# Quantised self-attention: row maxima turned and split group by group, first exponentials behind group 0 alone, the last group's maximum scores taken head by head between steps, one value bank in PSUM, the rounding of v on GpSimd

## The chip, the cores and the metric

The kernel is one program for one of the eight cores of a Trainium2 chip. The metric is the device time of one execution in microseconds. A core has TensorE (PE in the rows; its weight loads are PEld), VectorE (DVE), ScalarE (ACT), GpSimd (POOL) and SyncE (SP), each with its own queue of instructions, run in order. They meet on semaphores: an instruction adds to one with `then_inc`, another engine stands still at `wait_ge` until the count is there.

## What is computed

The block is cross-attention, then quantised self-attention, then a mixture of experts, on x of 8 x 128 tokens by 512. Only the middle part matters here:

```python
def _L0_attn_ref(query, key, value, in_w, in_b, out_w, out_b):   # query = layernorm(x), key and value unused
    X = fake_quant(einsum('lbe,fe->lbf', query, fake_quant(in_w)) + in_b)
    Q, K, V = split(X, 3, axis=-1)          # 16 heads of 32; L = 8, B = 128
    ...
    q = fake_quant(q / sqrt(HD))
    attn = softmax(einsum('bqd,bkd->bqk', q, k))
    heads = fake_quant(einsum('bqk,bkd->bqd', attn, v))
    y = heads_r @ Wo.T + out_b
    return fake_quant(y)
```

`fake_quant` divides by the largest absolute value of the whole tensor over 127, rounds, and multiplies back. Attention runs over L = 8 positions, for each of 128 batch rows and 16 heads apart.

## The kernel before

`quantised_self_attention` holds the stage. The 16 heads are in G = 4 groups f of GH = 4 heads j; one group fills the 128 partitions, 32 to a head. q and k lie transposed in `qk` (8 chunks of 128 x 1024: q of group f in chunk f, k in chunk 4 + f), v in `v_val` (8 tiles of 128 x 512, all groups side by side). PSUM, TensorE's output memory, is used as `pa` and `pb`, four banks of 128 x 512 each; `pt[0]` and `pt[1]` are banks 2 and 3 of `pb`.

The work between the scale of X (`x_scaled`) and the largest head value goes in two phases.

- **Maxima.** A group is quantised: k by two DVE instructions (`quantise_k`), q of groups 0 to 2 by four ACT instructions each, q of group 3 by four DVE instructions (`quantise_q`). `scores_for_max(f)` writes the mask (`half_l` by `half_r`) and 64 small matmuls into four banks (`pa` for even f, `pb` for odd), and DVE takes the largest score of each row, 128 x 2048 elements, into `mx`. After all four groups PE turns `mx` over (`m_turned`), and DVE splits it into `m_hi` and `m_lo`, two fp16 parts (`m_split`).
- **Steps.** s goes from 0 to 7; step s treats group s // 2, half s % 2 of its tokens. `scores_transposed(s)` writes mask, scores and minus the maximum into all of `pa`; ACT takes the exponential (2048 columns, `probs[s % 2]`); `times_v(s)` multiplies by v into bank s % 2 of `pb`, and ACT copies it to `heads` (`copy_heads`); `denominators(s)` sums the probabilities into `pt[0]`; DVE inverts (`invert`); `widen(s)` spreads the inverse over `pt[1]`; DVE multiplies and takes the largest (`normalise`).

The order of the work is written out by hand. PE runs `scores_transposed(s + 1)`, `times_v(s)`, `denominators(s)`, `widen(s - 1)` in each step. GpSimd rounds v of tiles 4 to 7 once three k groups are there (`v_late`), ACT those of tiles 0 to 3 after its q groups (`v_ready`).

Of the kernel before, what the change touches and what calls it, by code (L numbers as in the profile page):

```python
# [6 lines left out]
f16 = mybir.dt.float16  # L7
# [7 lines left out]
P = 128  # L15
# [3 lines left out]
EC = D // P  # L19
# [1157 lines left out]
def quantised_self_attention(nc, weights_q, wscale, in_b, out_b, w1, w2, stage, stage_in, shared, x1, x1_stats, ident, ident16):  # L1177
# [7 lines left out]
    with ExitStack() as c:  # L1185
# [26 lines left out]
        m_hi = sb("m_hi", [P, P], f16)  # L1212
        m_lo = sb("m_lo", [P, P], f16)
# [32 lines left out]
        v_ready, v_late = sem("v_ready2"), sem("v_late2")  # L1246
# [23 lines left out]
        with nc.Block() as block:  # L1270
# [11 lines left out]
            def _(gp):  # L1282
# [35 lines left out]
                gp.wait_ge(k_ready, G - 1)  # L1318
                for n, g in enumerate(range(4, B)):
                    gp.tensor_scalar(v_val[:, g, :], v_val[:, g, :], inv["x"][:, :], ROUND, ALU.mult, ALU.add).then_inc(v_late, 1)  # L1320
                    gp.wait_ge(v_late, 2 * n + 1)
                    gp.tensor_scalar(v_val[:, g, :], v_val[:, g, :], -ROUND, 1.0, ALU.add, ALU.mult).then_inc(v_late, 1)
# [8 lines left out]
            def _(act):  # L1331
# [19 lines left out]
                for f in range(G - 1):  # L1351
                    q_f = qk[:, f, :]
                    act.activation(q_f, q_f, ACT.Identity, bias=up, scale=inv["x"][:, :]).then_inc(q_step, 1)
                    act.wait_ge(q_step, 3 * f + 1)
                    act.activation(q_f, q_f, ACT.Identity, bias=down).then_inc(q_step, 1)
                    act.wait_ge(q_step, 3 * f + 2)
                    act.activation(q_f, q_f, ACT.Identity, bias=up, scale=scale["xq"][:, :]).then_inc(q_step, 1)
                    act.wait_ge(q_step, 3 * f + 3)
                    act.activation(q_int[:, f, :], q_f, ACT.Identity, bias=down).then_inc(q_ready, 1)

                for n in range(2):
                    v_n = v_val[:, 2 * n:2 * n + 2, :]
                    act.activation(v_n, v_n, ACT.Identity, bias=up, scale=inv["x"][:, :]).then_inc(v_ready, 1)
                    act.wait_ge(v_ready, 2 * n + 1)
                    act.activation(v_n, v_n, ACT.Identity, bias=down).then_inc(v_ready, 1)

                def copy_heads(s):
                    act.wait_ge(pv_done, s + 1)
                    act.activation(heads[:, s // 2, tokens(s)], pb[:, s % 2, :], ACT.Copy, scale=scale["x"][:, :]).then_inc(head_copied, 1)
# [24 lines left out]
            def _(dve):  # L1394
# [29 lines left out]

                split_xt(2)
# [42 lines left out]
                def quantise_k(f):  # L1468
                    k_f = qk[:, EC + f, :]
                    dve.tensor_scalar(k_f, k_f, inv["x"][:, :], ROUND, ALU.mult, ALU.add).then_inc(k_step, 1)  # L1470
                    dve.wait_ge(k_step, f + 1)
# [8 lines left out]

                quantise_k(0)
                quantise_k(1)
                quantise_k(2)
                for f in range(G):
                    if f == 1:
                        quantise_q(G - 1)
                    if f == 2:
                        quantise_k(G - 1)
                    dve.wait_ge(m_ready, f + 1)
                    dve.tensor_reduce(mx[:, :, 8 * f:8 * f + 8], (pa, pb)[f % 2][:, :, :].rearrange("p j (i n) -> p j i n", n=B * HT),  # L1490
                                      AX.X, ALU.max).then_inc(m_read, 1)

                dve.wait_ge(m_turned, 1)
                do(dve.tensor_scalar(m_round[:, :], pt[0][:, 0:P], 1.0 / 512.0, ROUND, ALU.mult, ALU.add))
                do(dve.tensor_scalar(m_hi[:, :], m_round[:, :], -ROUND, 1.0, ALU.add, ALU.mult))
                dve.scalar_tensor_tensor(m_lo[:, :], m_hi[:, :], -512.0, pt[0][:, 0:P], ALU.mult, ALU.add).then_inc(m_split, 1)
# [61 lines left out]
            def _(pe):  # L1558
# [48 lines left out]

                def scores_for_max(f):
                    out = (pa, pb)[f % 2]
                    pe.wait_ge(mask_ready, 1)  # L1610
                    if f >= 2:
                        pe.wait_ge(m_read, f - 1)
                    for j in range(GH):
                        rows = slice(HD * j, HD * j + HT + 1)
                        pe.matmul(out[:, j, :], half_l[rows, :], half_r[rows, :].unsqueeze(1).to_broadcast([HT + 1, 8, B * HT]),
# [805 lines left out]
```

## Time and profile before

| what | us |
|---|---|
| median of 3 runs | 1738.03 |
| the three runs | 1733.03, 1738.48, 1738.03 |
| the profiled execution | 1731.91 |
| its span (first to last instruction) | 1730.2 |
| from the scale of X (1166.05) to the largest head value (1228.19) | 62.1 |
| of that, before the first exponential (1189.81) | 23.8 |

The profiled execution is one run, 1.7 us longer than the span that the trace covers. A time such as 1189.81 is counted from the span's start. A row's idle time is that of the engine just before the instruction; it costs something only where the engine is the one for which all others wait.

### The profile page before, as it was taken

What the parts mean: (1) busy time and instruction counts of PE and PEld (TensorE: products, weight loads), DVE (VectorE), ACT (ScalarE), POOL (GpSimd) and SP (SyncE); (2) the same over time, 40 slices, a digit from 0 to 9 for tenths busy, and PEclk for the clock granted to TensorE, in tenths of its full rate; (3) what the DMA queues carried; (4) which work ended last, traced back from release to release, by engine and by line L of the source; (5) the groups of instructions that cost most, each with busy time, mean ns of one, the idle gap of its engine ahead of it and who ended that gap; (6) DMA issues with size and microseconds to landing.
All of it is one profiled execution on the core that took longest, in us unless ns stands there. A gap on an engine that the chain in (4) does not pass through costs nothing. (4 is left out here: it accounts for less than half of the span.)

```text
span 1730.2 us, 39796 instructions
## 1 busy us (share of the span) xinstructions
PE 1621.8 (94%) x17262; PEld 1109.3 (64%) x17262; DVE 1166.7 (67%) x1388; ACT 774.5 (45%) x979; POOL 466.9 (27%) x404
## 2 busy tenths in 40 slices
PE   6999999999999999999999999886569999999996
PEld 4666666666666666666766666664347777777774
DVE  5678568568567657657656766566787667666766
ACT  5355336335344444445435435447535344444441
POOL 2323312232232123123212247531024411101133
PEclk9999999999999999999999999996879999999998
DMA  6534343243234234233232235450048655645534
GB/s 245 126 108 111 68 108 86 62 123 86 47 98 111 47 87 114 56 87 92 59 105 74 57 87 141 104 209 3 2 140 279 203 180 182 201 171 181 192 127 110
DMA packets 102151, 202.04 MB, mean 117 GB/s; under 512 B 25739, under 2 KB 25739, under 8 KB 101850
## 3 DMA queue, kind: packets, MB, share of 16 engines
q1 hardware_dynamic: 91258, 169.49, 33.5%
q0 software_dynamic: 10720, 30.02, 6.1%
q8 instruction: 137, 2.24, 0.5%
q14 instruction: 36, 0.29, 0.0%
HBM read 127.36 MB, written 18.90 MB: 85 GB/s over the span
## 5 line engine op out<-in xcount | busy, mean ns | idle before, releaser
L656 DVE TENSOR_REDUCE mx<-sc 128x4 f32<-128x2048 f32 x128 | 293.1, 2290 | 65.4 <-PE sc L900 64.8
L861 PE MATMUL proj<-w_hi,ctx 128*128 128x256 f16 x2048 | 273.5, 278 | 12.6 <-ACT ctx L441 12.5
L489 ACT ACTIVATE stage_w<-sc 128x1024 f32<-128x1024 f32 x256 | 248.2, 1025 | 69.2 <-PE sc L935 68.5
L875 PE MATMUL proj<-ctx,w_hi 128*128 128x512 f16 x1024 | 253.6, 380 | 0.0
L861 PEld LDWEIGHTS proj<-w_hi,ctx 128*128 128x128 f16 x2048 | 193.2, 99 | 64.5 <-issue 40.1
L452 ACT ACTIVATE stage_w<-proj 128x512 f32<-128x512 f32 x128 | 76.4, 597 | 339.3 <-PE proj L861 339.3
L383 POOL TENSOR_TENSOR acc_g<-stage_w 128x1024 f32<-128x1024 f32 x31 | 74.0, 2389 | 472.2 <-ACT stage_w L489 472.1
L678 DVE TENSOR_TENSOR acc_v<-acc_v,stage_w 128x1024 f32<-128x1024 f32 x93 | 129.6, 1394 | 87.2 <-ACT stage_w L489 84.4
L1166 DVE SCALAR_TENSOR_TENSOR w_lo<-stage_w,w_hi 128x2048 f16<-128x2048 f32 x64 | 144.8, 2293 | 35.2 <-ACT w_hi L1160 35.1
L616 DVE SCALAR_TENSOR_TENSOR k_lo<-proj,k_hi 128x512 f16<-128x512 f32 x128 | 87.9, 687 | 117.9 <-ACT k_hi L461 117.0
L875 PEld LDWEIGHTS proj<-ctx,w_hi 128*128 128x128 f16 x1024 | 90.0, 98 | 116.5 <-issue 25.1
L861 PE MATMUL proj<-w_lo,ctx 128*128 128x256 f16 x1024 | 157.1, 277 | 1.2 <-DVE w_lo L604 1.2
L1947 ACT ACTIVATE hf<-ph 128x321 f32<-128x321 f32 x128 | 56.3, 440 | 208.1 <-PE ph L2220 190.5
L2236 PE MATMUL po<-h_lo,w_hi 128*128 128x321 f16 x496 | 149.3, 301 | 0.0
L2236 PE MATMUL po<-h_hi,w_hi 128*128 128x321 f16 x496 | 149.2, 301 | 0.0
L2236 PE MATMUL po<-h_hi,w_lo 128*128 128x321 f16 x496 | 149.2, 301 | 0.0
L935 PEld LDWEIGHTS sc<-qs,stage_w 97*128 97x128 f16 x2048 | 125.2, 98 | 31.2 <-ACT stage_w L489 2.5
L935 PE MATMUL sc<-qs,stage_w 97*128 97x128 f16 x2048 | 136.7, 220 | 3.8 <-DMA stage_w<-k_hi 1.6
L952 PE MATMUL po<-stage_w 128*32 128x128 f32 x4096 | 139.2, 277 | 0.0
L875 PE MATMUL proj<-ctx,w_lo 128*128 128x512 f16 x512 | 131.8, 380 | 0.0
L461 ACT ACTIVATE k_hi<-proj 128x512 f16<-128x512 f32 x128 | 76.5, 597 | 105.0 <-PE proj L875 101.8
L388 POOL TENSOR_TENSOR acc_g<-acc_g,stage_w 128x1024 f32<-128x1024 f32 x31 | 81.8, 2640 | 151.9 <-ACT stage_w L489 151.9
(344 smaller groups left out, 2492.5 us busy)
## 6 DMA issues: line engine op xcount, KB each, us to landing
stage_w<-in_w SPq DMA_DIRECT2D x64, 1024.0 KB, 5.6
ctx_stage<-in_ctxT SPq DMA_DIRECT2D x64, 512.0 KB, 4.4
stage_w<-k_hi SPq DMA_DIRECT2D x256, 128.0 KB, 2.4
stage_w<-k_lo SPq DMA_DIRECT2D x128, 128.0 KB, 2.4
wq_f<-in_wiT POOLq DMA_DIRECT2D x24, 256.0 KB, 4.2
xg<-xbuf POOLq DMA_DIRECT2D x28, 176.0 KB, 4.3
obuf<-o_sb POOLq DMA_DIRECT2D x28, 176.0 KB, 3.5
xbuf<-final SPq DMA_DIRECT2D x17, 256.0 KB
```

The source lines that it names most:

```text
L388: gp.tensor_tensor(acc_g[:, :], acc_g[:, :], probs[:, 3, :], ALU.add).then_inc(sum_g, 1)
L461: act.activation(k_hi[:, 512 * kb:512 * kb + 512], proj[where % 2][:, :], ACT.Copy, scale=1.0 / WSCALE).then_inc(proj_act, 1)
L489: act.activation(probs[:, u % 4, :], unit_scores(u), ACT.Exp, scale=1.0 / sqrt(HD)).then_inc(e_ready, 1)
L616: dve.scalar_tensor_tensor(k_lo[part], proj[where % 2][:, :], 1.0 / WSCALE, k_hi[part], ALU.mult, ALU.subtract).then_inc(k_low, 1)
L656: dve.tensor_reduce(mx[:, :, kb], sc[:, :, :], AX.X, ALU.max).then_inc(m_read, 1)
L678: dve.tensor_tensor(acc_v[:, :], acc_v[:, :], probs[:, (0, 0, 1, 2)[part], :], ALU.add).then_inc(sum_v, 1)
L861: last = pe.matmul(out, x_part[:, kb, e, col:col + P], w_part[:, 2, e, wv], start=term == 0 and e == 0, stop=term == 2 and e == EC - 1)
L875: last = pe.matmul(proj[at % 2][:, :], w_part[:, 1, e, P * (g % G):P * (g % G) + P], x_part[:, kb, e, :], start=term == 0 and e == 0, stop ...
L935: last = pe.matmul(sc[:, 2 * (u % 2) + i, P * j:P * j + P], ks[0:QKM, j, P * ck:P * ck + P], qs[0:QKM, 4 * g + j, :], start=True, stop=True)
L952: last = pe.matmul(po[HD * j:HD * j + HD, 0:T], v_sb[:, g // 2, ck, at:at + HD], probs[:, u % 4, 512 * i + P * j:512 * i + P * j + P], sta ...
L1166: dve.scalar_tensor_tensor(w_lo[:, s % NSPLIT], stage[:, s], WSCALE, w_hi[:, s % NSPLIT], ALU.mult, ALU.subtract).then_inc(stage_lo, 1)
L2236: last = pe.matmul(po[i][:, 0:CAP], w_part[:, s % NSPLIT, f, P * i:P * i + P], h_part[:, at, :], start=q == 0 and f == 0 and n == 0, stop= ...
```

## The change

The same values are computed, in another order and partly on other engines.

- DVE quantises q of group 0, then k of group 1; ACT quantises k of group 0, then q of groups 1 and 2. q and k of group 3 follow on DVE after the maxima of group 2.
- `mx` is set to zero at the start of the stage, and is turned and split three times (`turn_largest`, `split_largest`): after group 0, after group 2, after group 3. The parts go to two slots in the free region `xt2`.
- `scores_transposed(0)` and with it the first exponential wait for the first split alone. The maximum scores of groups 1 and 2 use `pb` (no longer two sets of banks in turn).
- The maximum scores of group 3 are made for one head at a time in one bank, `pb[:, 1]`, by 1 + 16 matmuls (`last_scores_for_max`), in the steps s = 1, 2, 3 and 4; DVE reads each by a 128 x 512 maximum (`largest_of_last`).
- `times_v` uses bank 0 of `pb` in every step, so it waits until the heads of the step before are copied.
- GpSimd rounds all eight tiles of v, as soon as q of group 0 is quantised; ACT none.

```diff
@@ GpSimd
-                gp.wait_ge(k_ready, G - 1)
-                for n, g in enumerate(range(4, B)):
+                gp.wait_ge(k_ready, 1)
+                for g in range(B):
...
@@ ScalarE
-                for f in range(G - 1):
+                k_0 = qk[:, EC, :]
+                act.activation(k_0, k_0, ACT.Identity, bias=up, scale=inv["x"][:, :]).then_inc(q_step, 1)
+                act.wait_ge(q_step, 1)
+                act.activation(k_int[:, 0, :], k_0, ACT.Identity, bias=down).then_inc(q_ready, 1)
+                for n, f in enumerate((1, 2)):
...
-                for n in range(2):
-                    v_n = v_val[:, 2 * n:2 * n + 2, :]
-                    act.activation(v_n, v_n, ACT.Identity, bias=up, scale=inv["x"][:, :]).then_inc(v_ready, 1)
-                    act.wait_ge(v_ready, 2 * n + 1)
-                    act.activation(v_n, v_n, ACT.Identity, bias=down).then_inc(v_ready, 1)
@@ VectorE
+                def largest_scores(f):
+                    dve.wait_ge(m_ready, f + 1)
+                    dve.tensor_reduce(mx[:, :, 8 * f:8 * f + 8], (pa, pb)[f > 0][:, :, :].rearrange("p j (i n) -> p j i n", n=B * HT),
+                                      AX.X, ALU.max).then_inc(m_read, 1)
+
+                def largest_of_last(j):
+                    dve.wait_ge(m_ready, G + j)
+                    dve.tensor_reduce(mx[:, j, 8 * G - 8:8 * G], pb[:, 1, :].rearrange("p (i n) -> p i n", n=B * HT),
+                                      AX.X, ALU.max).then_inc(m_read, 1)
+
+                def split_largest(n):
+                    turned = (pa[:, 0, 0:P], pb[:, 1, 0:P])[n > 0]
+                    dve.wait_ge(m_turned, n + 1)
+                    do(dve.tensor_scalar(m_round[:, :], turned, 1.0 / 512.0, ROUND, ALU.mult, ALU.add))
+                    do(dve.tensor_scalar(m_hi[:, n % 2, :], m_round[:, :], -ROUND, 1.0, ALU.add, ALU.mult))
+                    dve.scalar_tensor_tensor(m_lo[:, n % 2, :], m_hi[:, n % 2, :], -512.0, turned, ALU.mult, ALU.add).then_inc(m_split, 1)
...
+                quantise_q(0)
                 quantise_k(1)
+                largest_scores(0)
+                split_largest(0)
+                largest_scores(1)
                 quantise_k(2)
...
+                largest_scores(2)
+                quantise_k(G - 1)
+                split_largest(1)
+                quantise_q(G - 1)
...
                 for s in range(NS):
+                    if s == 4:
+                        largest_of_last(3)
                     invert(s)
+                    if 1 <= s < 4:
+                        largest_of_last(s - 1)
+                    if s == 4:
+                        split_largest(2)
                     if s:
                         normalise(s - 1)
@@ TensorE
+                def own_positions(out, j):
+                    rows = slice(HD * j, HD * j + HT + 1)
+                    pe.matmul(out, half_l[rows, :], half_r[rows, :].unsqueeze(1).to_broadcast([HT + 1, 8, B * HT]),
+                              start=True, stop=False, tile_position=(HD * j, 0))
+
+                def half_scores(out, f, i, h, j):
+                    at = slice(P * i + 64 * h, P * i + 64 * h + 64)
+                    rows = slice(HD * j, HD * j + HD)
+                    return pe.matmul(out[64 * h:64 * h + 64, 64 * i:64 * i + 64], q_int[rows, f, at],
+                                     k_int[rows, f, at], start=False, stop=i == 7, tile_position=(HD * j, 64 * h))
...
+                def last_scores_for_max(j):
+                    pe.wait_ge(m_read, 3 + j)
+                    if j == 0:
+                        pe.wait_ge(m_split, 2)
+                        pe.wait_ge(k_ready, G + 1)
+                    own_positions(pb[:, 1, :], j)
+                    for i in range(8):
+                        for h in range(2):
+                            last = half_scores(pb[:, 1, :], G - 1, i, h, j)
+                    last.then_inc(m_ready, 1)
+
+                def turn_largest(out, known):
+                    pe.wait_ge(m_read, known)
+                    pe.transpose(out, mx[:, :, :].rearrange("p j i -> p (j i)"), ident[:, :]).then_inc(m_turned, 1)
...
                     pe.wait_ge(e_ready, s + 1)
                     if s == 0:
-                        pe.wait_ge(v_ready, 4)
-                    if s == 1:
-                        pe.wait_ge(v_late, 8)
-                    if s >= 2:
-                        pe.wait_ge(head_copied, s - 1)
+                        pe.wait_ge(m_read, 3)
+                    else:
+                        pe.wait_ge(head_copied, s)
+                    if s < 2:
+                        pe.wait_ge(v_ready, B * (s + 1))
...
+                scores_for_max(0)
+                turn_largest(pa[:, 0, 0:P], 1)
+                scores_for_max(1)
                 scores_transposed(0)
+                scores_for_max(2)
                 for s in range(NS):
                     if s + 1 < NS:
                         scores_transposed(s + 1)
+                    if s == 0:
+                        turn_largest(pb[:, 1, 0:P], 3)
+                    if s == 4:
+                        last_scores_for_max(3)
                     times_v(s)
                     denominators(s)
+                    if 1 <= s < 4:
+                        last_scores_for_max(s - 1)
+                    if s == 4:
+                        turn_largest(pb[:, 1, 0:P], G + 3)
                     if s:
                         widen(s - 1)
```

On PE, from the maxima to the first step, the rows stood so before (`half_r,half_l` is the mask of `scores_for_max`, `k_int,wo_sb` its 64 matmuls, since q's integers lie in `wo_sb`; `ident,mx` is the turn; `mask_r,mask_l` opens `scores_transposed(0)`):

```order
L1615 MATMUL pa<-half_r,half_l 128x512 x4
L1625 MATMUL pa<-k_int,wo_sb 64x64 x64
L1615 MATMUL pb<-half_r,half_l 128x512 x4
L1625 MATMUL pb<-k_int,wo_sb 64x64 x64
L1615 MATMUL pa<-half_r,half_l 128x512 x4
L1625 MATMUL pa<-k_int,wo_sb 64x64 x64
L1615 MATMUL pb<-half_r,half_l 128x512 x4
L1625 MATMUL pb<-k_int,wo_sb 64x64 x64
L1692 MATMUL pb<-ident,mx 128x128
L1605 MATMUL pa<-mask_r,mask_l 128x512 x4
```

On PE at the same place they stand so in the changed kernel:

```order
L1626 MATMUL pa<-half_r,half_l 128x512 x4
L1632 MATMUL pa<-k_int,wo_sb 64x64 x64
L1663 MATMUL pa<-ident,mx 128x128
L1626 MATMUL pb<-half_r,half_l 128x512 x4
L1632 MATMUL pb<-k_int,wo_sb 64x64 x64
L1621 MATMUL pa<-mask_r,mask_l 128x512 x4
```

The turn and the first step have moved ahead of groups 2 and 3; after the step's matmuls come mask and 64 matmuls of group 2, and nothing of group 3.

On DVE, from the first k to the split of the maxima, these rows stood before (`ctx` is `qk`; L1470 and L1472 quantise k, L1476 to L1479 q of group 3, L1490 is the maximum of a group, L1494 to L1496 the split):

```order
L1470 TENSOR_SCALAR ctx<-ctx,inv_x 128x1024
L1472 TENSOR_SCALAR k_int<-ctx 128x1024 [waits k_step]
L1490 TENSOR_REDUCE mx<-pa 128x4x8 [waits m_ready2]
L1476 TENSOR_SCALAR ctx<-ctx,inv_x 128x1024
L1477 TENSOR_SCALAR ctx<-ctx,scale_xq 128x1024 [waits v_step2]
L1478 TENSOR_SCALAR ctx<-ctx 128x1024 [waits v_step2]
L1479 TENSOR_SCALAR wo_sb<-ctx 128x1024 [waits v_step2]
L1490 TENSOR_REDUCE mx<-pb 128x4x8 [waits m_ready2]
L1470 TENSOR_SCALAR ctx<-ctx,inv_x 128x1024
L1472 TENSOR_SCALAR k_int<-ctx 128x1024 [waits k_step]
L1490 TENSOR_REDUCE mx<-pa 128x4x8 [waits m_ready2]
```

In the changed kernel DVE's rows at that place are these (L1475 to L1478 quantise q of group 0, L1469 and L1471 k of group 1, L1482 is a group's maximum, L1493 to L1495 the split):

```order
L1475 TENSOR_SCALAR ctx<-ctx,inv_x 128x1024
L1476 TENSOR_SCALAR ctx<-ctx,scale_xq 128x1024 [waits v_step2]
L1477 TENSOR_SCALAR ctx<-ctx 128x1024 [waits v_step2]
L1478 TENSOR_SCALAR wo_sb<-ctx 128x1024 [waits v_step2]
L1469 TENSOR_SCALAR ctx<-ctx,inv_x 128x1024
L1471 TENSOR_SCALAR k_int<-ctx 128x1024 [waits k_step]
L1482 TENSOR_REDUCE mx<-pa 128x4x8 [waits m_ready2]
L1493 TENSOR_SCALAR xn<-pa 128x128 [waits m_turned]
L1494 TENSOR_SCALAR ctx_stage<-xn 128x128 [waits v_step2]
L1495 SCALAR_TENSOR_TENSOR ctx_stage<-ctx_stage,pa 128x128 [waits v_step2]
L1482 TENSOR_REDUCE mx<-pb 128x4x8 [waits m_ready2]
```

A group's q has moved ahead of everything, and a split stands between the first and the second maximum. Behind these rows DVE still has k of group 2, the maximum of group 2, k of group 3, the second split and q of group 3, and then the first `invert`.

In a step (here s = 1) PE has two rows more than before, those of `last_scores_for_max(0)` between the denominators (`probs,every`) and `widen` (`ot,ident`):

```order
L1701 MATMUL pb<-probs,v_val 32x128 x16
L1712 MATMUL pb<-probs,every 32x128 x16
L1626 MATMUL pb<-half_r,half_l 128x512
L1632 MATMUL pb<-k_int,wo_sb 64x64 x16
L1724 MATMUL pb<-ot,ident 32x128 x16
L1621 MATMUL pa<-mask_r,mask_l 128x512 x4
```

The mask is one matmul here and the scores sixteen, all with the rows of one head.

## Rows read from the trace of the kernel before

**Rows 1.** The page, parts 1 and 2: share of the span; 40 slices in tenths.

```profile
PE 1621.8 (94%) x17262; PEld 1109.3 (64%) x17262; DVE 1166.7 (67%) x1388; ACT 774.5 (45%) x979; POOL 466.9 (27%) x404
PEclk9999999999999999999999999996879999999998
```

**Rows 2.** Windows: stretch, length, busy us (instructions) by engine, PEclk, DMA share, GB/s.

```profile
1166.00:1188.00 22.00, 6.07 (x277) 3.51 (x281) 20.01 (x24) 19.96 (x17) 6.23 (x8) 0.50 0.01 1
1188.00:1198.00 10.00, 7.92 (x196) 6.05 (x192) 0.63 (x1) 4.54 (x3) 0.00 (x0) 0.51 0.01 2
1198.00:1228.00 30.00, 27.61 (x1004) 22.79 (x992) 17.89 (x24) 15.96 (x13) 0.00 (x0) 1.00 0.02 5
```

**Rows 3.** Timeline of the maxima: start, length, engine, line, what; idle before it, and releaser.

```profile
1166.05 1.24 ACT L1353 ACTIVATE ctx<-ctx,rounds_up,inv_x 128x1024 f32<-128x1024 f32 x1 [18.39 <-DVE scale_qx L1459]
1166.83 0.75 DVE L1470 TENSOR_SCALAR ctx<-ctx,inv_x 128x1024 f32<-128x1024 f32 x1
...
1171.07 0.79 PE L1625 MATMUL pa<-k_int,wo_sb 32*64 32x64 f16 x64 [3.68 <-ACT wo_sb L1359]
...
1171.80 0.61 PE L1615 MATMUL pb<-half_r,half_l 9*128 9x512 bf16 x4
1171.90 2.29 DVE L1490 TENSOR_REDUCE mx<-pa 128x32 f32<-128x2048 f32 x1 [0.81 <-PE pa L1625]
...
1180.37 1.23 ACT L1363 ACTIVATE v_val<-v_val,rounds_up,inv_x 128x1024 f32<-128x1024 f32 x1
...
1184.08 2.28 DVE L1490 TENSOR_REDUCE mx<-pb 128x32 f32<-128x2048 f32 x1
1185.10 1.28 ACT L1375 ACT_TABLE_LOAD   x1
...
1186.42 0.47 PE L1692 MATMUL pb<-ident,mx 128*128 128x128 f32 x1 [3.60 <-DVE mx L1490]
...
1187.86 0.61 PE L1605 MATMUL pa<-mask_r,mask_l 17*128 17x512 bf16 x4 [0.97 <-DVE m_lo L1496]
```

**Rows 4.** Groups by line and shape, 1166 to 1188: count, busy us, mean ns.

```profile
L1320 POOL TENSOR_SCALAR v_val<-v_val,inv_x 128x512 f32<-128x512 f32 x4 | 3.2, 803 | 21.3 <-DVE k_int L1472 21.3
L1322 POOL TENSOR_SCALAR v_val<-v_val 128x512 f32<-128x512 f32 x4 | 3.1, 774 | 0.3
L1470 DVE TENSOR_SCALAR ctx<-ctx,inv_x 128x1024 f32<-128x1024 f32 x4 | 3.0, 746 | 0.0
L1472 DVE TENSOR_SCALAR k_int<-ctx 128x1024 f16<-128x1024 f32 x4 | 2.8, 694 | 0.1
...
L1476 DVE TENSOR_SCALAR ctx<-ctx,inv_x 128x1024 f32<-128x1024 f32 x1 | 1.1, 1142 | 0.0
L1478 DVE TENSOR_SCALAR ctx<-ctx 128x1024 f32<-128x1024 f32 x1 | 1.1, 1066 | 0.0
```

**Rows 5.** Timeline of the first two steps.

```profile
1189.81 1.97 ACT L1375 ACTIVATE probs<-pa,scale_qx 128x2048 f32<-128x2048 f32 x1 [3.42 <-PE pa L1645]
1191.83 0.61 PE L1605 MATMUL pa<-mask_r,mask_l 17*128 17x512 bf16 x4 [2.08 <-ACT probs L1375]
...
1193.65 1.94 PE L1661 MATMUL pb<-probs,v_val 128*32 128x128 f32 x32
...
1197.23 0.61 PE L1605 MATMUL pa<-mask_r,mask_l 17*128 17x512 bf16 x4
...
1198.45 1.08 PE L1661 MATMUL pb<-probs,v_val 128*32 128x128 f32 x32
...
1199.35 1.06 PE L1672 MATMUL pb<-probs,every 128*32 128x128 f32 x32
```

**Rows 6.** Timeline, a later step, and the last row of the steps.

```profile
1204.33 0.68 ACT L1369 ACTIVATE ctx<-pb,scale_x 128x512 f32<-128x512 f32 x1
...
1206.23 1.08 PE L1661 MATMUL pb<-probs,v_val 128*32 128x128 f32 x32
...
1227.47 0.69 DVE L1414 TENSOR_REDUCE tile_max<-ctx 128x1 f32<-128x512 f32 x1
```

More of the change, by code:

```diff
@@ L1423, in largest_qk @@
                     absmax(tile_max[:, j // 2, 2 * c + j % 2:2 * c + j % 2 + 1], of_pairs(qk[:, 2 * j:2 * j + 2, :], c), AX.XY)
+                steps.did(dve.memset(mx[:, :, :], 0.0))
                 split_xt(2)
@@ L1608, in scores_for_max @@
                 def scores_for_max(f):
-                    out = (pa, pb)[f % 2]
+                    out = (pa, pb)[f > 0]
                     pe.wait_ge(mask_ready, 1)
-                    if f >= 2:
-                        pe.wait_ge(m_read, f - 1)
+                    if f == 2:
+                        pe.wait_ge(m_read, 2)
                     for j in range(GH):
-                        rows = slice(HD * j, HD * j + HT + 1)
-                        pe.matmul(out[:, j, :], half_l[rows, :], half_r[rows, :].unsqueeze(1).to_broadcast([HT + 1, 8, B * HT]),
-                                  start=True, stop=False, tile_position=(HD * j, 0))
@@ L1617, in scores_for_max @@
-                    pe.wait_ge(k_ready, f + 1 if f < G - 1 else G + 1)
-                    if f < G - 1:
-                        pe.wait_ge(q_ready, f + 1)
+                        own_positions(out[:, j, :], j)
+                    pe.wait_ge(k_ready, f + 1)
+                    pe.wait_ge(q_ready, f + 1)
                     for i in range(8):
                         for h in range(2):
-                            at = slice(P * i + 64 * h, P * i + 64 * h + 64)
                             for j in range(GH):
-                                rows = slice(HD * j, HD * j + HD)
-                                last = pe.matmul(out[64 * h:64 * h + 64, j, 64 * i:64 * i + 64], q_int[rows, f, at],
-                                                 k_int[rows, f, at], start=False, stop=i == 7, tile_position=(HD * j, 64 * h))
+                                last = half_scores(out[:, j, :], f, i, h, j)
@@ L1646, in scores_transposed @@
                                                  pick[rows, n, HD * j + at:HD * j + at + 1].to_broadcast([HD, P]),
-                                                 m_part[rows, :], start=False, stop=i == 3 and n == 1, tile_position=(HD * j, 0))
+                                                 m_part[rows, (0, 1, 1, 0)[s // 2], :], start=False, stop=i == 3 and n == 1, tile_position=(HD * j, 0))
                     last.then_inc(s_ready, 1)
@@ L1660, in times_v @@
                             at = P * (s // 2) + HD * j
-                            last = pe.matmul(pb[HD * j:HD * j + HD, s % 2, P * i:P * i + P],
+                            last = pe.matmul(pb[HD * j:HD * j + HD, 0, P * i:P * i + P],
                                              v_val[:, 4 * (s % 2) + i, at:at + HD],
```

43 lines of the change are left out of this document (15 added, 28 removed).

## The prediction

> **What bounds the kernel now.** I read the page first. TensorE is busy for 94% of the span, and its clock stands at the full level of 2.4 GHz except around slice 28 [rows 1]. A stretch in which PE is not the limit is there, and it is the one changed. The windows put numbers on it: from 1166 to 1188 PE works 6.1 of 22 us at half clock (0.50, which is 1.2 GHz), while VectorE has 20.0 and ScalarE 20.0 of 22; from 1188 to 1198 PE has 7.9 of 10 us, still at 0.51; from 1198 to 1228 it is at 1.00 and busy 27.6 of 30 [rows 2]. DMA share is 0.01 to 0.02 throughout, so no transfer bounds this stage [rows 2].
>
> The timeline says why the first exponential is so late. ScalarE makes three q groups in a row, 1166.05 to 1180.37, 4.77 us each, and PE waits for each (3.68 us before the first). VectorE has four maxima of 2.3 us, four k groups and one q group; its last maximum ends at 1186.36, and only then come the turn, the split and, at 1187.86, the first step [rows 3]. The exponential starts at 1189.81 [rows 5]. From then on the steps form a chain on PE. The second denominators start at 1199.35 and the last row of the steps ends at 1228.16 [rows 5, 6]: what moves 1199.35 moves the end.
>
> **The change, part by part.** I lay the new order out with the durations of before, starting from 1166.
>
> *Group 0.* VectorE starts q of group 0 at 1166.83 in place of k: two instructions of 0.75 and two of 0.69 [rows 4], with three gaps of 0.04 some 3.0 us, so 1169.85. ScalarE's k of group 0 is half a q group, 2.4 us, ready at 1168.5, hidden. PE's 64 matmuls follow, before at 1171.07 [rows 3], now at 1169.9, done at 1170.7.
>
> *First split.* VectorE has k of group 1 next. Two instructions are 1.44 us alone [rows 4], but GpSimd now starts on v at 1170.0. Only q of group 3 ran beside GpSimd before: 1.14 for the form that takes 0.75 [rows 4]. That is 0.39 more for one instruction; I take 0.33 each, so 2.1 us, to 1171.95. Then the maximum of group 0, 2.29, to 1174.25. Turn and split took 1.44 us from 1186.42 to 1187.86 [rows 3], so the parts are ready at 1175.75; PE meanwhile makes the scores of group 1 (0.4 for the mask, 0.79, after 0.2 for the turn) until 1175.8. The first step stands on PE at 1175.8 instead of 1187.86. Its scores took 1.95 us to the exponential [rows 3, 5], 1177.75. But ScalarE is busy: from 1168.5 two q groups of 4.77, 1178.05, and the table load of 1.28 [rows 3] that lay in a wait before. First exponential: 1179.35 to 1181.35, 10.5 us earlier. ScalarE sets that.
>
> *Groups 1 and 2.* VectorE: maximum of group 1 from 1175.85 to 1178.15, k of group 2 (2.1) to 1180.25, PE 0.8 to 1181.05, maximum of group 2 to 1183.4, k of group 3 (GpSimd is about done) to 1184.85, second split 0.9 to 1185.75, q of group 3 3.0 to 1188.75, then the first `invert`, about 1.0, to 1189.75. PE: second step's scores from 1181.4 (1.82, as 1191.83 to 1193.65 [rows 5]) to 1183.2; `times_v(0)` waits for the maximum of group 2 and for the turn, 1183.7; it and the denominators take 3.58 at half clock (1193.65 to 1197.23 [rows 5]), 1187.3; then step 2's scores (1.2) and `times_v(1)` (0.9), both as in [rows 5], to 1189.4. `denominators(1)` waits for the first inverse, 1189.85, where before it stood at 1199.35. **That is 9.5 us.** The clock rose about 1197.8 before, some 6 us into unbroken work from 1191.83 [rows 2, 5]. If PE here is still at 1.2 GHz after 1187.3, those two pieces take 1.8 and 1.5, the denominators start at 1190.6, and 8.75 are left. I take 9.3.
>
> *v on GpSimd.* Eight tiles at a mean of 0.80 + 0.77 us [rows 4] are 12.6 us, 1170.0 to 1182.6. They are wanted at 1183.7 (first four) and 1188.5. Even a pair at 2.0 for every tile ends at 1186. So nothing on the path; the price is the VectorE instructions above. ScalarE's 4.7 us of v (1180.37 to 1185.10 [rows 3]) go, and only the table load moves up with it.
>
> *Group 3 in the steps.* Four times PE gets a mask of one matmul and 16 score matmuls, at full clock, in a chain that is PE-bound. Nothing before runs like this, since all four heads went side by side. From below: four masks together take 0.6 at half clock, 64 matmuls 0.79 [rows 3], so at least 0.2 for a 512-column mask at double clock plus a quarter of 0.79: 0.4. From above: one head alone as slow as all four at half clock, 0.4 + 0.79: 1.2. One head has two column halves and no neighbours, so I lean to the middle below, 0.6, since the clock is double: 4 x 0.6 = 2.4 (1.6 to 4.8). The third turn adds 0.1. VectorE's four reads of 128 x 512 are 0.69 as L1414 [rows 6] and the third split 0.9; it is busy 17.9 of 30 us there [rows 2], with 0.7 more in a step, so it stays under PE.
>
> *One value bank.* `times_v(s)` now needs the copy of s - 1. In a step of before that copy ends at 1205.01 and `times_v` starts at 1206.23 [rows 6]: 1.2 us of margin, no cost. *`mx` to zero* is 128 x 128, at a stage start where VectorE waits for ScalarE: nothing.
>
> The sum: -9.3 + 2.4 + 0.1 = **-6.8 us**. The profiled execution would go from 1731.91 (span 1730.2) to 1725.1. The runs have a median of 1738.03, 6.1 above it, and spread over 5.5 us; I subtract the same 6.8 from the median: 1731.2.
>
> **The rivals.**
>
> *GpSimd stops VectorE more.* The row shows 0.39 us more for one overlapped instruction and GpSimd's own pair lengthened to a mean of 1.57 [rows 4]. If instead each of the six k instructions waited for a whole GpSimd instruction (0.7), VectorE's chain would be 6 x 0.7 = 4.2 longer where I took 1.3, and 2.7 of it reach the first inverse: net -4.1, 1733.9. Against it stands that q of group 3, whose instructions ran beside GpSimd at 1.07 and 1.14. The Trainium skill, "SBUF — State Buffer", section "Who interferes with whom", has this as an exclusive lock: a two-port VectorE instruction and a GpSimd one do not share, the later one blocks fully. By that rule the price depends on who comes first, up to the rival's 4.2; the trace agrees that the two lengthen each other, at 0.39.
>
> *The group-3 pieces cost more.* At the upper bound, 1.2 each, the steps give back 4.8: net -4.4, 1733.6. For it: 16 matmuls share one head's 32 rows, so weights and data of successive ones may not overlap; against: 64 took only 0.79 at half clock.
>
> *It comes out slower.* The single value bank makes every step wait. The margin is 1.2 us [rows 6]. Seven steps wait for it, so if a step's copy comes x later than the margin allows, the cost is 7x. To undo 6.8 and add 5.2 (0.3%), x = 1.7, that is, the copy 2.9 us later against `times_v` than now. What could do it is ScalarE, but it has 2.65 us of work in a step of 3.9 (two of them from 1198.45 to 1206.23 [rows 5, 6]); there is room of over 1 us. From x = 1.0 on the gain is gone. At x = 1.7 the time is 1743.
>
> *Nothing is gained at the end.* If something later than the stage set its end, the 6.8 would be lost, 1738.0. DMA at 0.01 to 0.02 [rows 2] leaves nothing that I see to wait for.
>
> **How the numbers follow.** Main case 0.62, likely 1729.5 to 1733 as the clock and the group-3 pieces fall (-8.5 to -5); GpSimd 0.12; costly pieces 0.15; slower 0.05; nothing 0.06. Within 0.3% (5.2 us, about what a measurement of this kernel tells from no change) are 1732.8 to 1743.2: both middle rivals, the last one, and a sixth of the main case whose size is less than hoped. Faster: 0.56. Same: 0.39. Slower: 0.05. The range takes -8.5 with 3 us for the spread of the runs at the lower end, 1726.5, and covers the gain lost almost wholly at the upper, 1737.
>
> **What the profile would show.** Right: first exponential near 1179.4 after a table load at 1178; `denominators(1)` near 1190 with a short wait for the first inverse; in steps 1 to 4 a gap of about 0.6 between denominators and `widen`; the last maximum of heads near 1221.4; after it nothing changed. Wrong: VectorE's k instructions at 1.4 and more; PE waiting for `head_copied` in the steps; the clock still at 0.5 beyond 1191; pieces of group 3 above 1 us.

## The result, and the profile after

The changed kernel takes 1725.59 us (median of 5 runs, 1724.75 to 1728.27) against 1735.2 of the kernel before in the same session (median of 5, 1732.83 to 1738.48; three of the five are the runs that the prediction started from). The ratio is 0.9946, with a 95% interval of 0.993 to 0.9962: 9.4 us faster, 6.6 to 12.1. The forecast was 6.8 us faster, 1731.2, with a range of 1726.5 to 1737.0. The direction holds, and 6.8 lies within the interval of the gain, near its lower end; the absolute time lies 0.9 us under the range.

The profiled execution of after took 1728.27 us, the slowest of its five, with a span of 1726.3. The page, busy shares and clock in 40 slices, as [rows 1]:

```profile
PE 1624.6 (94%) x17264; PEld 1109.9 (64%) x17264; DVE 1172.4 (68%) x1400; ACT 767.1 (44%) x973; POOL 471.7 (27%) x412
PEclk9999999999999999999999999997879999999998
```

The page cannot tell the two kernels apart, since the stage is 3% of the span. The windows of the stage say more (columns as [rows 2]; this execution reached the scale of X at 1168.06, 2.0 us later than before's):

```profile
1168.00:1188.00 20.00, 11.05 (x374) 7.67 (x374) 17.65 (x26) 17.58 (x14) 11.71 (x16) 0.53 0.01 2
1188.00:1200.00 12.00, 11.21 (x418) 8.87 (x414) 8.61 (x12) 5.78 (x6) 0.00 (x0) 1.00 0.02 4
1200.00:1224.00 24.00, 20.33 (x683) 16.17 (x675) 14.71 (x22) 10.23 (x9) 0.00 (x0) 1.00 0.02 4
```

In the first 20 us PE now does 11.1 us of work, before 6.1 in 22: the scores of the first two steps and the first `times_v` and `denominators` are in there. The clock is full in the window from 1188 on, that is, 20 us after the scale of X, before 32. The timeline of after:

```profile
1168.06 1.24 ACT L1352 ACTIVATE ctx<-ctx,rounds_up,inv_x 128x1024 f32<-128x1024 f32 x1 [18.40 <-DVE scale_qx L1458]
...
1171.75 0.75 DVE L1469 TENSOR_SCALAR ctx<-ctx,inv_x 128x1024 f32<-128x1024 f32 x1
...
1172.00 1.05 POOL L1320 TENSOR_SCALAR v_val<-v_val,inv_x 128x512 f32<-128x512 f32 x1 [20.11 <-DVE wo_sb L1478]
1172.53 1.07 DVE L1471 TENSOR_SCALAR k_int<-ctx 128x1024 f16<-128x1024 f32 x1
...
1180.03 1.28 ACT L1373 ACT_TABLE_LOAD   x1
...
1181.33 1.97 ACT L1373 ACTIVATE probs<-pa,scale_qx 128x2048 f32<-128x2048 f32 x1
...
1189.96 0.95 DVE L1512 RECIPROCAL ot<-pb 128x128 f32<-128x128 f32 x1
...
1190.97 1.08 PE L1712 MATMUL pb<-probs,every 128*32 128x128 f32 x32 [0.79 <-DVE ot L1512]
...
1191.98 0.39 PE L1626 MATMUL pb<-half_r,half_l 9*128 9x512 bf16 x1
...
1192.30 0.44 PE L1632 MATMUL pb<-k_int,wo_sb 32*64 32x64 f16 x16
...
1192.67 1.07 PE L1724 MATMUL pb<-ot,ident 32*32 32x128 f32 x32
...
1208.25 0.40 PE L1621 MATMUL pa<-mask_r,mask_l 17*128 17x512 bf16 x4 [0.56 <-DVE ctx_stage L1495]
...
1223.46 0.69 DVE L1412 TENSOR_REDUCE tile_max<-ctx 128x1 f32<-128x512 f32 x1
```

Marks are counted from here on from the start of the stage, ScalarE's first row after the scale of X (1168.06 here; 1166.05 before, [rows 3]). The exponential follows its table load at +13.3 (before +23.8, [rows 5]), the second denominators stand at +22.9 behind a wait for the first inverse (before +33.3), a piece of group 3 takes 1191.98 to 1192.67, 0.69 us, and the stage ends at +56.1 (before +62.1, [rows 3, 6]). So the stage is 6.0 us shorter, while the medians differ by 9.6 and the two spans by 3.9. The 3.9 are these 6.0 less the 2.0 us by which this execution reached the stage later, and less 0.1 behind it. Why the start moves, and what the gain is apart from such spread, is what the experiments are for.

### The profile page after: what moved, and what is told of

Same layout as the page of the kernel before. It is cut to its first block and busy times, and to the rows that moved or that the text cites. A ratio compares the mean times of both kernels' runs of the same rounds, so it can differ in the third digit from the quotient of the medians.

```text
span 1726.3 us, 39816 instructions
## 1 busy us (share of the span) xinstructions
PE 1624.6 (94%) x17264; PEld 1109.9 (64%) x17264; DVE 1172.4 (68%) x1400; ACT 767.1 (44%) x973; POOL 471.7 (27%) x412
## 5 line engine op out<-in xcount | busy, mean ns | idle before, releaser
L1994 ACT ACTIVATE hf<-ph 128x321 f32<-128x321 f32 x128 | 56.1, 438 | 208.2 <-PE ph L2267 190.6
```

## The experiments

"Stage" is the time from the start mark to the end of the last head maximum, in the profile of one execution. "Stalls" are the time lost in PE's steps to waits with no releaser: what a step takes over the regular 3.89 us, or 4.57 with a piece of group 3.

| kernel | 1st exp. | 2nd denom. | stage | stalls in it | median us (runs) | ratio to before |
|---|---|---|---|---|---|---|
| before | 23.8 | 33.3 | 62.1 | 0.9 | 1735.2 (5) | |
| before_again | 23.8 | 32.5 | 61.9 | 1.5 | 1731.93 (12) | 0.9995 (0.9982 to 1.0007) |
| after | 13.3 | 22.9 | 56.1 | 1.7 | 1725.59 (5) | 0.9946 (0.993 to 0.9962) |
| after_again | 13.3 | 22.9 | 54.4 | 0 | 1726.19 (6) | 0.9958 (0.9942 to 0.9974) |
| after_third | 13.3 | 22.9 | 54.5 | 0.1 | 1726.74 (6) | 0.9954 (0.9938 to 0.997) |
| twice | 13.3 | 22.9 | 57.1 | 0 | 1729.86 (10) | 0.9977 (0.9963 to 0.999) |
| v_on_act | 17.9 | 27.7 | 59.1 | 0 | 1728.9 (10) | 0.9982 (0.9969 to 0.9994) |
| no_v | 13.3 | 22.7 | 56.2 | 2.1 | 1727.32 (10) | 0.9977 (0.9966 to 0.9989) |
| only_v | 24.4 | 32.9 | 62.2 | 1.5 | 1734.32 (10) | 1.0011 (0.9997 to 1.0024) |
| at_once | 13.3 | 31.0 | 60.5 | 1.7 | 1734.3 (12) | 1.0011 (1.0001 to 1.0022) |
| at_once_again | 13.3 | 30.6 | 60.9 | 2.5 | 1735.51 (12) | 0.9993 (0.9977 to 1.0008) |
| reordered | 13.3 | 22.2 | 54.7 | 1.6 | 1727.36 (12) | 0.9971 (0.9958 to 0.9983) |
| reordered_again | 13.3 | 22.4 | 55.5 | 2.2 | 1726.43 (6) | 0.9948 (0.9935 to 0.9961) |
| warm | 13.3 | 22.3 | 54.6 | 1.4 | 1726.46 (6) | 0.9949 (0.9937 to 0.9962) |

Each ratio is to the kernel before as it was timed in the same set of runs. Behind the first five runs there are three such sets, in which the kernel before had medians of 1733.57 (29 runs), 1732.44 (35) and 1734.09 (17); over all 81 the median is 1733.4.

**after_again** and **after_third**: the changed kernel, unaltered.

> The changed kernel once more, unaltered. The stage is counted from the first ScalarE row after the scale of X to the end of the last head maximum: 62.1 us in the profile of before, 56.1 in that of after, so -6.0, while the medians differ by 9.6 and the two spans by only 3.9. Theory A (the stage's gain is fixed by its waits, the rest is spread of the executions elsewhere): the stage again takes 55.5 to 57 us, and the medians of this call differ by 6 to 9 us. Theory B (the first profile caught the change at a bad moment, the typical gain inside the stage is near 9): the stage takes 53 to 54 us.

> The changed kernel a third time, beside the next three on one chip. Stages so far: 56.1 and 54.4 us, the 1.7 between them being two stalls of PE in which nothing is waited for (1.2 near +42.6 and 0.5 near +47), in step with fetches of instructions. Theory A: the marks at +13.3 (first exponential), +21.9 (first inverse) and +22.9 (second denominators) repeat to 0.05 us, the end lies at 54.4 plus the stalls, 0 to 2 us; mean time 6 to 8 us under before. Theory B (the gain depends on the build's upstream part): the marks repeat, but the mean is off by more than 2 us from the -7 so far.

All marks up to the second denominators repeat to 0.05 us. The stage is 54.4 and 54.5; what the first profile had more is two stalls. The 54.4 lie in neither of the ranges expected for after_again, 55.5 to 57 and 53 to 54; the medians of that set differ by 7.4, inside its 6 to 9. For after_third the expectation held, with 0.1 of stalls and a mean 7.4 under before's. PE's timeline of after shows the larger:

```profile
1210.15 0.82 PE L1712 MATMUL pb<-probs,every 128*32 128x128 f32 x18
1211.76 0.64 PE L1712 MATMUL pb<-probs,every 128*32 128x128 f32 x14 [0.79 <-issue]
```

The same denominators in after_again, again PE's timeline:

```profile
1211.36 0.40 PE L1621 MATMUL pa<-mask_r,mask_l 17*128 17x512 bf16 x4 [0.64 <-DVE ctx_stage L1495]
1212.36 1.08 PE L1701 MATMUL pb<-probs,v_val 128*32 128x128 f32 x32
1213.26 1.06 PE L1712 MATMUL pb<-probs,every 128*32 128x128 f32 x32
```

One is cut in the middle after 18 of 32 matmuls, with nothing that it waits for; the other runs through. From 1208.5 to 1212.5 the DMA view of after has a single packet, and it is one of instructions:

```profile
DMA packets 1, 0.02 MB, mean 4 GB/s; under 512 B 0, under 2 KB 0, under 8 KB 0
## 3 DMA queue, kind: packets, MB, share of 16 engines
q8 instruction: 1, 0.02, 1.6%
```

That a fetch lies near a stall says little by itself, since in the steps one comes every 3.2 to 5.4 us. Its time says more. These are the GB/s of 40 slices of 0.2 us in the DMA view, counted from +35.9 in both, first of after, then of after_again:

```profile
GB/s 0 82 0 0 0 0 0 0 41 0 0 0 0 0 0 0 0 0 0 0 0 0 0 0 0 0 82 0 0 0 0 0 0 0 0 0 0 0 0 0
GB/s 0 0 0 0 0 0 0 0 41 0 0 0 0 0 0 82 0 0 0 0 0 0 0 0 0 0 0 0 0 0 0 0 0 0 82 0 0 0 0 0
```

(The 41 are a fetch on another queue.) PE is at the same point in both: `scores_transposed(6)` begins at +40.19. The fetch on q8 stands at +41.1 in after, 5.0 us behind the one before it, and at +38.9 in after_again, 3.3 behind. no_v, the other profile with a large stall there, is cut after the same 18th matmul and has its fetch at +41.5, 5.4 behind. A late fetch, and PE out of code 1 to 2 us behind it, fits all three profiles. It was not made to happen, nothing of the kind is shown for the smaller stalls, and what makes a fetch late is open. Taken over both profiles of before and all three of after, the stage is worth 5.8 to 7.7 us.

**before_again**: the kernel before, unaltered.

> The kernel before, unaltered, timed against itself. Theory A: the ratio to itself lies off 1 by up to 0.2%, the stage takes 62 to 62.5 us again, and the time up to the stage differs from the first profile's 1166.05 by 1 to 3 us though no instruction there is another. Theory B (executions repeat to within 1 us outside the stage): start of the stage within 0.5 us of 1166.05 and ratio within 0.05% of 1.

Ratio 0.9995, stage 61.9, start of the stage at 1167.60, 1.55 later than in the first profile, without a change of code: Theory A, with the stage 0.1 under its 62 to 62.5. The trace shows how such a difference arises, first at the same eight matmuls of cross-attention. PE's timeline of before:

```profile
330.16 3.65 PE L1021 MATMUL misc<-wo_sb,ot 128*128 128x512 f32 x8
```

PE's timeline of before_again:

```profile
330.21 5.35 PE L1021 MATMUL misc<-wo_sb,ot 128*128 128x512 f32 x8
```

The windows view (columns as [rows 2]) of two of these microseconds, of before:

```profile
332.00:334.00 2.00, 2.00 (x7) 0.79 (x6) 1.26 (x2) 0.00 (x0) 0.00 (x0) 1.00 0.00 0
```

and of before_again:

```profile
332.00:334.00 2.00, 2.00 (x3) 0.67 (x2) 1.16 (x1) 0.00 (x0) 0.00 (x0) 0.50 0.00 0
```

In both PE has just waited 1.6 to 1.7 us for a DMA. In one the clock stays at 2.4 GHz, in the other it falls to 1.2, and the eight matmuls take 1.7 us more. These 1.7 us are not the 1.55 at the stage, though: at 416 it is before whose clock is low (0.52), and from 420 on the two run level to 0.1 us. At 689 before_again loses 1.7 us again, at 822 before does (0.57), and they are level once more at 826. What reaches the stage is the last such place. There the clock stood at 1.2 GHz in both from 1106 on, behind three waits of PE of 0.7 to 1.1 us, and rose later in before_again. The windows of before and of before_again:

```profile
1110.00:1112.00 2.00, 2.00 (x56) 1.77 (x52) 0.00 (x0) 1.21 (x2) 1.74 (x3) 1.00 0.23 72
1110.00:1112.00 2.00, 2.00 (x32) 1.57 (x25) 0.00 (x0) 0.00 (x0) 1.75 (x3) 0.50 0.22 72
```

From there to the stage the 1.54 us stay. So each execution meets such losses of 1.5 to 1.8 us at several places, and how many it meets differs. Over all profiles the stage starts between 1166.05 and 1173.58. Over the 64 executions of before in the first two of the three sets the time goes with the mean granted clock by some 1.2 us for each 0.001 of it (correlation -0.7). So the clock carries a good part of the spread of several us in single runs.

**twice**: each piece of group 3 made twice.

```diff
+                    for again in range(2):
                         own_positions(pb[:, 1, :], j)
                         ...
```

> Mask and scores of group 3 are made twice in each of the four pieces; the second makes the same values. In the profile of after a piece takes 0.69 us on PE (0.32 mask, 0.37 scores). Theory A (each piece stands in full on the chain of the steps): the stage grows by 4 x 0.69 = 2.8 us to 58.9. Rival (the pieces lie partly in waits of PE that would be there anyway): it grows by less than 1.5 us.

The stage is 57.13 against 54.38 of after_again, both without stalls: 2.75 us more. A piece costs its full length on the chain. PE's timeline of twice:

```profile
1197.05 0.39 PE L1626 MATMUL pb<-half_r,half_l 9*128 9x512 bf16 x1
1197.37 0.44 PE L1632 MATMUL pb<-k_int,wo_sb 32*64 32x64 f16 x16
1197.73 0.38 PE L1626 MATMUL pb<-half_r,half_l 9*128 9x512 bf16 x1
```

0.32 for the mask, 0.36 for the sixteen.

**v_on_act**: ScalarE rounds tiles 0 to 3 of v again.

```diff
-                for g in range(B):                                   # GpSimd
+                for n, g in enumerate(range(4, B)):
...
+                for n in range(2):                                   # ScalarE, after q of group 2
+                    v_n = v_val[:, 2 * n:2 * n + 2, :]
...
```

> As after, but ScalarE rounds v of tiles 0 to 3 after its q groups, as in the kernel before, and GpSimd only tiles 4 to 7. Theory A (ScalarE sets the first exponential, so its 4.7 us of v come straight onto the path): the first exponential starts 4.7 us later, and some of it is swallowed since times_v(0) waits for the maximum of group 2 only until 3.6 us after that exponential's end; the stage grows by 3 to 4.5 us. Rival (VectorE's chain hides it): it grows by under 1 us.

The first exponential is 4.6 us later, the second denominators 4.8, the stage 4.75 (59.13 against 54.38), a little more than expected. Two things cancel in it. The wait of 0.6 to 0.8 us for the first inverse is gone, so that much is swallowed; and `denominators(0)` runs at 1.2 GHz here, 1.93 us, where it took 1.05 to 1.08 in the profiles of after:

```profile
1190.34 1.93 PE L1720 MATMUL pb<-probs,every 128*32 128x128 f32 x32
1192.21 0.46 PE L1627 MATMUL pa<-mask_r,mask_l 17*128 17x512 bf16 x4
```

In the changed order ScalarE does set the first exponential, and v on GpSimd is worth 4.75 us of stage, most of the 6.0 to 6.8 that the change gains without stalls.

**only_v**: the kernel before with v on GpSimd, and nothing else.

```diff
-                for n, g in enumerate(range(4, B)):
+                for n, g in enumerate(range(B)):
...
-                for n in range(2):
-                    v_n = v_val[:, 2 * n:2 * n + 2, :]
```

> The kernel before with one part of the change: GpSimd rounds all of v, ScalarE none. Before, ScalarE ends v at +19.0 and the first exponential, +23.8, waits for VectorE's maxima. Theory A (the part is worth nothing by itself): ScalarE's 4.7 us were hidden, GpSimd now also overlaps k of group 3, and the first exponential comes 0 to 0.8 us later; stage 62 to 63 us. Rival (freeing ScalarE is where the gain is): the stage is 2 us or more shorter than 62.1.

First exponential 0.7 us later, stage 62.2, ratio 1.0011 (0.9997 to 1.0024). In the old order the same edit is worth nothing or a little less, since VectorE's maxima come last. v_on_act is the other half, the new order with v where it was: without stalls its stage is 1 to 2 us shorter than before's. Together they make 6.0 to 6.8, so most of the gain belongs to neither alone.

**no_v**: leaves out the rounding of v, so GpSimd does not run beside VectorE; the values of v stay as they are, and the kernel computes something else.

```diff
-                for g in range(B):
-                    gp.tensor_scalar(v_val[:, g, :], ...)
```

> As after, but v is not rounded at all (the two GpSimd instructions of each of the eight tiles are left out, so the values of v stay unrounded and unscaled). Stage marks of after: first exponential +13.3 us, first inverse +21.9. In its profile four VectorE instructions that quantise k ran beside GpSimd at 0.75, 1.07, 0.92 and 0.98 where they take 0.75 and 0.69 alone: 0.85 us too much in all. Theory A (GpSimd takes that and no more): the first exponential stays at +13.3, the first inverse comes 0.6 to 0.9 us earlier, at +21.1, and the stage ends as much earlier. Rival (GpSimd blocks VectorE by whole instructions, 0.7 us each): 2 us and more.

The first inverse starts at +21.3, 0.6 us earlier. The end gains only 0.2 to 0.3 us (54.1 without stalls), less than expected: PE no longer waits for the inverse, and the second denominators stand behind PE's own work, where the clock rose later here. In this profile the window from 1184 to 1190 is at 0.62, in after's at 0.76:

```profile
1184.00:1190.00 6.00, 6.00 (x173) 4.95 (x165) 5.62 (x11) 2.66 (x2) 0.00 (x0) 0.62 0.01 3
```

So GpSimd costs VectorE 0.6 us up to the first inverse, not 2, and half of that or less reached the end.

**at_once** and **at_once_again**: group 3's maxima in one go, before `times_v(0)`.

```diff
                     if s == 0:
-                        turn_largest(pb[:, 1, 0:P], 3)
+                        scores_for_max(3)
+                        turn_largest(pb[:, 1, 0:P], 4)
-                    if s == 4:
-                        last_scores_for_max(3)
...
```

> As after, but group 3's maximum scores are made at once, four banks, before times_v(0), and turned with those of groups 1 and 2; no piece stands in the steps. Theory A (the pieces cost 2.75 us and their turn and split about 0.9, but taking group 3 ahead puts q of group 3, 3.0, PE's 0.8 and a maximum of 2.3 us ahead of times_v(0)): the first denominators come some 6.5 us later, 3.6 us are saved in the steps, the stage ends 2.5 to 4 us later than after, at 57 to 60. Rival (the pieces are a bad bargain, the gain comes from group 0 first alone): the stage is no longer than in after, 54.4 to 56.1.

> The version with group 3 at once, a second time. Its stage was 60.5 us with 1.7 of stalls, 1.5 shorter than before's, yet its median was 1.9 us longer than before's. Theory A (spread of the time ahead of the stage; the stage decides): mean within 0 to 2 us under before's here. Theory B (something outside the stage is slower in this build): mean over before's again by 1 us or more, with the start of the stage late or the tail after it longer than 502 us.

The second denominators come at +31.0, 8.1 us later, the steps are 3.6 shorter, the stage is 60.5, some 4.5 over after_again without stalls. That is more than the 2.5 to 4 expected: the first denominators are 7.3 us later (at +26.5), not 6.5, and run at 1.2 GHz, 1.93 us. The steps gain the 3.6 expected. VectorE's timeline shows q of group 3 and the maximum standing in front:

```profile
1193.58 0.69 DVE L1478 TENSOR_SCALAR wo_sb<-ctx 128x1024 f16<-128x1024 f32 x1
1195.16 2.29 DVE L1482 TENSOR_REDUCE mx<-pb 128x32 f32<-128x2048 f32 x1 [0.89 <-PE pb L1627]
```

The whole kernel takes as long as before's (means +1.2 and -0.9 us), though the stage is 1 to 1.5 us shorter. The second mean lies in Theory A's 0 to 2 us under. Both profiles reach the stage late, at 1173.1 and 1173.6, but so do those of twice (1173.1) and reordered_again (1172.8), while the three of after lie between 1167.8 and 1171.2. Late starts are nothing special to this kernel; whether it draws them more often stays open.

**reordered** and **reordered_again**: three moves on VectorE to fill waits.

```diff
                 largest_scores(0)
+                quantise_k(2)
                 split_largest(0)
                 largest_scores(1)
-                quantise_k(2)
...
-                quantise_q(G - 1)
+                do(dve.tensor_scalar(q_f, q_f, -ROUND, scale["xq"][:, :], ALU.add, ALU.mult))
+                invert(0)
+                do(dve.tensor_scalar(q_f, q_f, ROUND, 1.0, ALU.add, ALU.mult))
...
                     times_v(s)
+                    if s == 4:
+                        turn_largest(pb[:, 1, 0:P], G + 3)
                     denominators(s)
```

> As after, with three moves on VectorE: k of group 2 ahead of the first split (it fills the wait for the turn), the first inverse between the second and third instruction of q of group 3, and in step 4 the third turn ahead of the denominators and its split ahead of the inverse. In after's profiles PE waits 0.6 to 0.8 us for the first inverse, 0.56 to 0.64 for the third split, and the maximum of group 2 starts 0.9 after VectorE is free. Theory A (these waits stand on the path): the stage is 1.3 to 2.2 us shorter than the 54.4 of after without stalls, 52.2 to 53.1; the median falls by about 0.1%, which the timing may not tell. Rival (another wait takes their place at once, the key tie being ScalarE's first exponential): under 0.6 us.

> The reordered version a second time, paired with after on one chip. Its first stage was 54.7 us with 1.65 of stalls, so 53.05 without, 1.3 less than after; yet its mean was 5.5 us under before against 7.1 for after on another chip. Theory A (that was the chip and the spread, the stage decides): mean 0.5 to 2 us under that of after in this call. Theory B (the build moves stalls or clock falls elsewhere and eats the gain): mean equal to or above after's.

The marks do what was expected: second denominators 0.5 to 0.7 us earlier, no wait for the third split, 53.05 and 53.3 us of stage without stalls. But stalls came to 1.6 and 2.2 us, and on one chip reordered_again and after_third have the same mean, 1727.5 (medians 1726.43 and 1726.74). That is Theory B. In the profiles the waits for VectorE are gone and stalls stand in the steps instead; that the one brought the other is not shown, since after itself had between none and 1.7 us of stalls.

**warm**: reordered, with eight matmuls more in PE's wait for the first maximum.

```diff
                 scores_for_max(0)
+                for n in range(8):
+                    pe.matmul(pb[:, n % 4, :], qo_q[:, 0, 0:P], qo_q[:, 0, :], start=True, stop=True)
```

> As reordered, with 8 more matmuls of 128 x 512 on PE (their output in pb is overwritten) where it waits from +4.6 to +7.8 us for the first maximum. The clock stood at 1.2 GHz until about +19 us in all profiles. Theory A (the clock rises near +9 and the head of the stage runs on at 2.4 GHz through short waits): second step's scores take 1.0 in place of 1.8, times_v(0) and its denominators 1.9 in place of 3.5, and the second denominators start at about +21.2, where VectorE sets them, in place of 22.2; the stage is 1 us shorter, near 52 without stalls. Rival (the clock falls again in the waits up to +15, nothing comes of it, the extra matmuls only delay the turn by up to 0.4): stage unchanged or 0.4 longer.

Its windows show a clock that rises and falls again:

```profile
1170.00:1175.00 5.00, 3.38 (x71) 1.66 (x72) 4.90 (x6) 4.90 (x6) 3.09 (x4) 0.50 0.00 0
1175.00:1180.00 5.00, 3.46 (x124) 1.75 (x122) 4.90 (x7) 4.88 (x5) 4.74 (x7) 0.78 0.02 3
1180.00:1185.00 5.00, 3.25 (x121) 2.24 (x121) 3.47 (x3) 3.02 (x2) 3.88 (x7) 0.56 0.01 3
```

The first step still had the high clock, and lost it behind the next wait. PE's timeline of warm:

```profile
1178.41 0.40 PE L1626 MATMUL pa<-mask_r,mask_l 17*128 17x512 bf16 x4 [1.02 <-DVE ctx_stage L1495]
1180.70 0.61 PE L1631 MATMUL pb<-half_r,half_l 9*128 9x512 bf16 x4 [1.22 <-DVE mx L1482]
```

Four masks take 0.40 us at 2.4 GHz and 0.61 at 1.2. The first step gains nothing by its clock, since ScalarE sets the first exponential; from 1180.7 on it is 1.2 GHz again, for the second step too, and the second denominators stay at +22.3. The rival was right: the stage without stalls is 53.2.

## Why the prediction was right, and where not

**First exponential.** Forecast +13.3, measured +13.27 or +13.28 in all three profiles, with ScalarE last as said. v_on_act shows that it is the limiter.

**Second denominators.** Forecast +23.8, or 9.5 us earlier, and 9.3 taken; measured +22.9, which is 10.4 us earlier than before's first profile and 9.6 than its second, where the clock rose one piece of work sooner. VectorE's chain was 0.8 us shorter than laid out. GpSimd was one reason: k of groups 1 and 2 took 1.82 and 1.90 us where 2.1 was taken for each, and no_v puts the whole contention at 0.6. The allowance for a late clock was not needed: in after `denominators(0)` took 1.05 us, not the 1.9 of half clock, so PE was ready early and waited 0.79 us for the inverse. The rival of whole-instruction blocking (2.7 us) is out. By the exclusive lock of the Trainium skill, "SBUF — State Buffer", section "Who interferes with whom", an instruction can wait for the other engine's one; the rows agree in kind: VectorE's 1.07 in place of 0.69 stands behind a GpSimd instruction that began 0.5 us earlier, and that one, itself begun behind a VectorE instruction, took 1.05, while this VectorE instruction kept its 0.75. The price was 0.2 to 0.4 us for each of three k instructions, where the rival counted 0.7 for each of six.

**Pieces of group 3.** Forecast 0.6 each, 2.4 in all; measured 0.69 and 2.75, shown on the path by twice. The costly-pieces rival is out. The wait for the third split, 0.56 to 0.64 us, was put at nothing ("it stays under PE"): `split_largest(2)` stands behind an inverse on VectorE, and `scores_transposed(6)` needs it. The third turn took 0.26, not 0.1.

**One value bank.** No wait for `head_copied` in any step, as forecast.

**Sum.** Forecast -9.3 + 2.4 + 0.1 = -6.8. Measured without stalls, after_again against before_again (61.9 less 1.5): -9.6 for the head, +3.6 for pieces, turn and split, -6.0. Against before's first profile (62.1 less 0.9), from which the forecast was made, it is -10.4 and +3.6, which is -6.8. That this is the forecast to a tenth is luck: the head gave 1.1 us more than forecast, the steps cost 1.1 more. With the stalls as they fell, the stage is worth 5.8 to 7.7 us. The three timings of the whole give ratios of 0.9946, 0.9958 and 0.9954, at 1733 some 9.4, 7.3 and 8.0 us, each with an interval of about 2.8 us to either side; all contain 6.8.

**The step that failed** is "I subtract the same 6.8 from the median: 1731.2", and with it the lower end of 1726.5, which hangs on the same 1738.03. The term was the base, not the gain. The median of three runs was high: with two runs more it was 1735.2, and the 81 later executions of the same kernel have a median of 1733.4, with only six at 1738.03 or above. The changed kernel stayed where it was, at 1725.59, 1726.19 and 1726.74. From 1733.4 the same sum gives 1726.6; from the profiled execution the prediction itself had 1725.1, 0.5 us from the result, and it gave no reason for taking the median, 6.1 above, instead. The three runs gave a warning: two at 1738 and one at 1733 are 5 us apart, almost the size of the forecast gain, and the 3 us allowed for the spread were half of the 6.1 that it had seen. Why those three were high is not in the record, as no trace of them was kept; that falls of the clock at many places can do it is read from before_again.

Two slips in the working change nothing of this. `times_v` at half clock takes 1.7 us from start to start (1193.65 to 1195.36 before), not 1.5, so the late-clock case would leave 8.5, not 8.75. And with a sixth of the main case the chance of "same" adds up to 0.43 and that of "faster" to 0.52, not 0.39 and 0.56.

## What to carry to other kernels

An engine freed is worth what it is last for: the same move of v to GpSimd bought 4.7 us in the new order and nothing in the old, so a move of work and the order that exposes it are costed together. Where a forecast gain is as small as the spread of the runs, take the stage's marks from the trace for the size, and for the absolute time a base from all runs there are, with the profiled one among them. Marks ahead of the stage are no measure of a change behind them: in the same kernel they lie 1.5 us and more apart. And where waits are filled, check that the end moved and not only the mark: reordered's marks came 0.5 to 0.7 us earlier, and the time stayed.

## What the runs showed of the hardware

- A fall of the clock to 1.2 GHz after a wait of PE of 1.6 to 1.7 us comes in some executions and not in others, and costs 1.7 us over eight 128 x 512 f32 matmuls (3.65 against 5.35 us). Two executions of one kernel differed so at five places, by 1.5 to 1.8 us each; four cancelled in pairs, and the last, at 1110, is the 1.54 us by which before_again reached the stage later.
- PE stalls of 0.1 to 1.5 us stand inside runs of small matmuls; up to 2.5 us in a stage, none in another execution of the same kernel. The two large ones with a piece of code fetched shortly before (after, no_v) have this fetch 5.0 and 5.4 us behind the one before it, where after_again has 3.3.
- Eight large matmuls in a wait lift the clock for a few us only: 0.78 in one window of 5 us, 0.56 in the next, after waits of 1.0 and 1.2 us.
- VectorE and GpSimd lengthen each other's instructions, and the one that begins first keeps its time: VectorE 0.75 of 0.75, then GpSimd 1.05 of 0.69, then VectorE 1.07 of 0.69. VectorE's maximum of 128 x 2048 out of PSUM took its 2.27 to 2.29 us beside GpSimd as well.
